# Keys and queries projected transposed and stacked through DRAM, in a fused attention and mixture-of-experts kernel

## What is computed

```python
q = (ln(x) @ Wq + bq)                      # 256 x 256, 16 heads of 16
k = concat([side @ Wk + bk, ctx], axis=1)  # 512 keys
v = concat([side @ Wv + bv, ctx], axis=1)
attn = softmax(einsum('bhqd,bhkd->bhqk', q, k) / 4)
x = x + (attn @ v) @ Wp + bp
h = ln(x)
cw = normalised(softmax(h @ w_router) * softmax(h @ w_gating / 0.1))   # 8 experts, all of them
x = x + sum_e cw[e] * ((silu(h @ w_gate[e]) * (h @ w_up[e])) @ w_down[e])   # hidden width 1024
```

## Time and profile before

| | |
|---|---|
| median of 3 runs | 2773.96 us (2772.17 to 2774.82) |
| profiled execution, its time | 2771.69 us |
| its span | 2769.6 us, granted TensorE clock 0.994 on average |
| busy share TensorE, VectorE, ScalarE, GpSimd | 98%, 73%, 61%, 62% |
| bytes moved | 252 MB |

### The profile page before, as it was taken

How to read it: one execution, slowest core, us unless ns; L and a number is a source line. 1 busy time by engine, 2 the same in 40 slices (tenths; PEclk the granted TensorE clock), 3 DMA queues, 4 the chain that set the end, 5 groups by cost and what they waited for, 6 DMA issues and landing times.

```text
span 2769.6 us, 48148 instructions
## 1 busy us (share of the span) xinstructions
PE 2721.2 (98%) x16465; PEld 2228.0 (80%) x16465; DVE 2009.8 (73%) x3254; ACT 1689.5 (61%) x3241; POOL 1720.9 (62%) x1886
## 2 busy tenths in 40 slices
PE   7789999999999999999999999999999999999998
PEld 5568888888888888888888888888888888888887
DVE  6877777768777777777777778677776867665554
ACT  7766666666666666565666666666666665544443
POOL 6766566666666566666665666665665665654554
PEclk9999999999999999999999999999999999999999
DMA  2113233332333322333232322323323233333332
GB/s 69 40 54 101 76 99 96 92 101 79 99 93 93 102 84 88 96 95 100 83 95 83 106 89 85 103 81 109 94 80 101 78 99 92 93 107 116 104 104 83
DMA packets 251280, 252.32 MB, mean 91 GB/s; under 512 B 15904, under 2 KB 242848, under 8 KB 251040
## 3 DMA queue, kind: packets, MB, share of 16 engines
q1 hardware_dynamic: 251040, 249.25, 29.6%
HBM read 240.66 MB, written 8.52 MB: 90 GB/s over the span
## 4 chain that ended last, share of the span: by engine, by line
PE 92%; issue 3%; DVE 2%; ACT 2%; POOL 1%; DMA 0%; SPq 0%; POOLq 0%; ACTq 0%; DVEq 0%
PE ps_t L670 25%; PE ps_o L704 24%; PE ps_s L670 24%; PE ps_s L764 4%; PE ps_t L774 4%; PE ps_m L549 3%; PE ps_a L746 2%; PE ps_a L748 2%; PE ps_m L607 1%; PE ps_m L567 1%; PE ps_m L622 1%; PE ps_m L614 1%; ACT Pt L928 0%; DVE Pt_lo L1154 0%; DVE negmax L1146 0%
## 5 line engine op out<-in xcount | busy, mean ns | idle before, releaser
L949 DVE SCALAR_TENSOR_TENSOR hf<-hf,ps_s 128x512 f32<-128x512 f32 x512 | 350.2, 684 | 401.5 <-ACT hf L788 400.3
L794 ACT ACTIVATE h_hi<-ps_t 128x512 fp32r<-128x512 f32 x512 | 306.2, 598 | 451.1 <-DVE ps_t L956 451.1
L961 DVE TENSOR_TENSOR h_lo<-ps_t,h_hi 128x512 fp32r<-128x512 f32 x512 | 353.0, 689 | 213.9 <-ACT h_hi L794 207.6
L788 ACT ACTIVATE hf<-ps_s 128x512 f32<-128x512 f32 x512 | 306.3, 598 | 329.8 <-PE ps_s L670 327.7
L1185 POOL TENSOR_TENSOR wg_lo<-stage_w,wg_hi 128x512 fp32r<-128x512 f32 x256 | 337.4, 1318 | 265.5 <-ACT wg_hi L801 264.7
L1250 POOL TENSOR_TENSOR Pt_lo<-Pt 128x512 f16<-128x512 f32 x256 | 289.7, 1132 | 197.9 <-ACT Pt L928 197.0
L704 PE MATMUL ps_o<-h_lo,wd_hi 128*128 128x512 f32 x1024 | 399.9, 390 | 0.0
L704 PE MATMUL ps_o<-h_hi,wd_hi 128*128 128x512 f32 x1024 | 398.5, 389 | 0.9 <-DVE h_lo L961 0.9
L704 PE MATMUL ps_o<-h_hi,wd_lo 128*128 128x512 f32 x1024 | 398.4, 389 | 0.0
L956 DVE TENSOR_TENSOR ps_t<-hf,ps_t 128x512 f32<-128x512 f32 x512 | 356.4, 696 | 48.1 <-PE ps_t L670 7.5
L1185 POOL TENSOR_TENSOR wd_lo<-stage_w,wd_hi 128x512 fp32r<-128x512 f32 x256 | 332.1, 1297 | 87.5 <-ACT wd_hi L801 87.5
(11 more groups left out here) (192 smaller groups left out, 5092.4 us busy)
## 6 DMA issues: line engine op xcount, KB each, us to landing
stage_w<-in_L_ffn_w_gate_dram SPq DMA_DIRECT2D x256, 256.0 KB, 2.7
stage_w<-in_L_ffn_w_up_dram SPq DMA_DIRECT2D x256, 256.0 KB, 3.0
stage_w<-in_L_ffn_w_down_dram SPq DMA_DIRECT2D x256, 256.0 KB, 2.7
cwb<-d_cw SPq DMA_DIRECT2D x64, 256.0 KB, 3.6
X<-in_x_dram SPq DMA_DIRECT2D x32, 256.0 KB, 3.2
C<-in_fside_BxSxS_dram SPq DMA_DIRECT2D x16, 256.0 KB, 3.0
KVM<-in_ctx_dram SPq DMA_DIRECT2D x16, 256.0 KB, 2.8
d_x<-X SPq DMA_DIRECT2D x16, 256.0 KB, 2.9
```

The costliest lines, as they stand in the source:

```text
L788: act.activation(hf[:], ps_g[:], ACT.Tanh, scale=0.5).then_inc(tanh_done, 1)
L794: act.activation(h_hi[f % FC][:], ps_u[:], ACT.Copy).then_inc(hh_done, 1)
L949: dve.scalar_tensor_tensor(out=hf[:], in0=hf[:], scalar=1.0, in1=ps_g[:], op0=ALU.add, op1=ALU.mult).then_inc(gate_done, 1)
L961: dve.tensor_tensor(h_lo[f % FC][:], ps_u[:], h_hi[f % FC][:].bitcast(F32), ALU.subtract).then_inc(hl_done, 1)
```

## The change

1. Keys and queries are projected with features on partitions (`project_across`: weights stationary, 256 tokens moving), so no transposition is needed. ScalarE evacuates the high part with the bias added from a per-partition column `bT`, VectorE the low part. The factor 1/4 goes into `Wq`'s split. Memory keys are transposed once per batch (item `m`, four transposes). Values have an item of their own (`v`).
2. The low and high parts are written to DRAM (`d_k`, `d_q`), 4 transfers per batch, and read back into the rows of `KTs` and `QTs`, for 4 pairs at once: 3 transfers of 32 partitions for keys, 6 of 16 partitions and one that clears the maxima's rows for queries, two groups per batch. `QTs` now holds all 8 pairs. Rows: slots of 32 (two heads of 16), the last 32 rows for the maxima. SP issues all of it.
3. `kT` and `qq` items are gone, `qm` (maxima only) stays. The other items stand at other steps. `kstack`, `qstack`, `KVM`'s key part, `QF` are gone.
4. In steps without feed-forward VectorE takes the low part of `Pt` (and the router's small work) ahead of the step's item and maximum, not behind.
5. Prologue: GpSimd clears all of `QTs`, a transfer fills the ones rows of `KTs`, `KEEP_BUSY` is set anew.

```diff
-        ITEMS = [(0, "kT", 5, 0), (1, "kT", 6, 0), (2, "qq", 1, 0), (3, "cT", 0, 1), (4, "kT", 7, 0), (5, "aT", 0, -1),
-                 (6, "qq", 2, 0), (8, "o", 0, -1), (9, "kv", 0, 1), (10, "qq", 3, 0), (11, "kv", 1, 1), (13, "xT", 0, 1),
-                 (14, "qq", 4, 0), (15, "x2T", 0, -1), (16, "q", 0, 1), (17, "lg", 0, -1), (18, "qq", 5, 0), (19, "kT", 0, 1),
-                 (20, "kT", 1, 1), (21, "y", 0, 0), (22, "qq", 6, 0), (23, "cwT", 0, -1), (24, "y", 1, 0), (25, "kT", 2, 1),
-                 (26, "qq", 7, 0), (27, "kT", 3, 1), (28, "kT", 4, 1), (30, "qq", 0, 1)]
-        FIRST_AT = {"cT": (1,), "xT": (2,), "kv": (4, 6), "q": (9,)}
+        ITEMS = [(1, "cT", 0, 1), (2, "qm", 1, 0), (4, "k", 0, 1), (5, "aT", 0, -1), (6, "qm", 2, 0), (8, "o", 0, -1),
+                 (9, "v", 0, 1), (10, "qm", 3, 0), (11, "xT", 0, 1), (12, "m", 0, 1), (13, "q", 0, 1), (14, "qm", 4, 0),
+                 (15, "x2T", 0, -1), (17, "lg", 0, -1), (18, "qm", 5, 0), (21, "y", 0, 0), (22, "qm", 6, 0),
+                 (23, "cwT", 0, -1), (24, "y", 1, 0), (26, "qm", 7, 0), (30, "qm", 0, 1)]
+        FIRST_AT = {"cT": (1,), "xT": (2,), "k": (4,), "m": (6,), "q": (7,), "v": (9,)}
...
+                eng.wait_ge(const_ready, CONSTS)
+                eng.dma_start(KTs[TOP:P].bitcast(F32), key_rows[TOP:P].unsqueeze(1).broadcast_to([ROWS, PAIRS, NK])).then_inc(rows_in, 16)
+            def store_keys(turn, d):
+                turn.wait(eng, k_l, d, 2)
+                turn.wait(eng, m_l, d, 1)
+                for n, part in enumerate((kT_hi, kT_lo)):
+                    eng.dma_start(d_k[turn.b + d, n].rearrange("(c p) n -> p c n", p=P), part[:].bitcast(F32)).then_inc(k_out.sem, 16)
...
+            def place_keys(turn, d, g):
+                turn.wait(eng, k_out, d, 32)
+                turn.wait(eng, t_ps, d - 1, 2 * OCT * (g + 1))
+                for slot, part in enumerate((0, 1, 0)):
+                    eng.dma_start(KTs[slot * ROWS:(slot + 1) * ROWS, g * GP:(g + 1) * GP, :].bitcast(F32),
+                                  d_k[turn.b + d, part, bass.ds(g * P, P)].rearrange("(a r) n -> r a n", r=ROWS)).then_inc(k_in[g].sem, 16)
+            def place_queries(turn, d, g):
+                turn.wait(eng, q_out, d, 32)
+                turn.wait(eng, t_ps, d - 1, 2 * OCT * (g + 1))
...
+                for slot, part in enumerate((0, 0, 1)):
...
+                    src = d_q[turn.b + d, part, bass.ds(g * P, P)].rearrange("(a h r) n -> h r a n", h=2, r=HD)
+                    for h in range(2):
+                        r = slot * ROWS + h * HD
+                        eng.dma_start(QTs[r:r + HD, pairs, h, :].bitcast(F32), src[h]).then_inc(q_in[g].sem, 32 if last and h == 1 else 16)
...
+                    first = turn.b == -1
+                    if turn.has(1) and step == (10 if first else 14):
+                        store_keys(turn, 1)
+                    if turn.has(1) and step == (10 if first else 15):
+                        store_queries(turn, 1)
+                    if turn.has(1) and step == (11 if first else 17):
+                        place_keys(turn, 1, 0)
+                    if turn.has(1) and step == (11 if first else 19):
+                        place_queries(turn, 1, 0)
+                    if turn.has(0) and step == 1:
+                        place_keys(turn, 0, 1)
+                    if turn.has(0) and step == 3:
+                        place_queries(turn, 0, 1)
...
-            KEEP_BUSY = {(-2, 0): 13, (-1, 2): 10, (-1, 4): 6, (-1, 19): 10, (-1, 22): 2, (-1, 24): 8}
+            KEEP_BUSY = {(-2, 0): 13, (-1, 2): 10, (-1, 4): 6, (-1, 24): 36}
...
+            def project_across(ps, col, a, w):
+                (act, act_lo), (wt, wt_lo) = a, w
+                for m in range(DC):
+                    n, last = 0, 3 * DC - 1
+                    for tok, half in ((act, wt), (act, wt_lo), (act_lo, wt)):
+                        for c in range(DC):
+                            mm = pe.matmul(ps[:, m * N:(m + 1) * N], half[:, c, col + m * P:col + (m + 1) * P], tok[:, c, :],
+                                           start=(n == 0), stop=(n == last))
+                            n += 1
+                return mm
...
-                        if i % 4 == 0:
-                            turn.wait(pe, kT_done, d, h // 2 + 1)
-                            turn.wait(pe, qT_done, d, 2 * (h // 2) + 2)
+                        if i % (4 * GP) == 0:
+                            g = i // (4 * GP)
+                            if turn.b + d == 0:
+                                pe.wait_ge(rows_in, 16)
+                            turn.wait(pe, k_in[g], d, k_in[g].per)
+                            turn.wait(pe, q_in[g], d, q_in[g].per)
...
+                    if f is None:
+                        router_weights(turn, step)
+                        low_part(turn, step)
                     name, k, d, one, _ = misc(turn, step)
...
+                    if turn.b == -1 and step == 4:
+                        dve.wait_ge(b_in[0], 32)
+                        dve.tensor_scalar(bT[:, 0], bT[:, 0], SCALE, None, ALU.mult).then_inc(b_scaled, 1)
...
-            pool.memset(kstack[:, :, 2, 3:HD].bitcast(F32), 0.0).then_inc(const_ready, 1)
-            pool.memset(kstack[:, :, 2, 0:3].bitcast(F32), 1.0).then_inc(const_ready, 1)
-            pool.memset(qstack[:, :, 2, :].bitcast(F32), 0.0).then_inc(const_ready, 1)
+            pool.memset(key_rows[:], 0.0).then_inc(rows_clear, 1)
+            pool.memset(QTs[:].bitcast(F32), 0.0).then_inc(const_ready, 1)
```

More of the change, by code:

```diff
@@ L30 @@
 P = 128
-SLOTS = 4
+ROWS = 32
 LN_EPS = 1e-5
@@ L296, in released @@
                 return [] if turn.closed is None else [(y_done, turn.closed * GB + k + 1)]
[L297 to L303, removed]
+            count, nth = {"qm": (qm_done, 2 * k + 2), "k": (k_l, 2), "m": (m_l, 1), "v": (v_done, 1), "xT": (xT_l, 1),
+                          "cT": (cT_l, 1), "aT": (aT_l, 1), "x2T": (x2T_l, 1), "q": (q_l, 2), "o": (x1_done, 1),
+                          "lg": (ldif_done, 1), "cwT": (cwT_done, 1)}[name]
             return [(count.sem, (b + d) * count.per + nth)] if turn.has(d) else []
@@ L597, in do_misc @@
                         pe.wait_ge(w_low, 2)
-                    project(ps, 0, 2 * D, (cT_hi, cT_lo), k, (wkv_hi, wkv_lo)).then_inc(kv_ps.sem, 1)
-                elif name == "kT":
+                    for t in range(QT):
+                        mm = project(ps, t * D, D, (cT_hi, cT_lo), t, (wkv_hi[:, :, D:2 * D], wkv_lo[:, :, D:2 * D]))
+                    mm.then_inc(v_ps.sem, 1)
+                elif name == "qm":
                     if turn.b == -1:
[L601 to L621, removed]
-                            mm = pe.transpose(ps[:, N + t * P:N + (t + 1) * P].bitcast(F32R),
-                                              stack_block(qstack, t, pair), ident_r[:])
-                        mm.then_inc(qT_ps.sem, 1)
+                        pe.wait_ge(ident_done, 3)
+                    turn.wait(pe, mq_l, d, k + 1)
+                    for t in range(QT):
+                        mm = pe.matmul(ps[:, t * P:(t + 1) * P], mq[k % 2][:, t, :], ident_b[:], start=True, stop=True)
+                    mm.then_inc(qm_ps.sem, 1)
                 elif name == "aT":
@@ new lines, in body @@
+                    if name in ("k", "q"):
+                        full, hi, out_c, b_at, used = {"k": (k_ps, kT_hi, k_h, 1, k_out), "q": (q_ps, qT_hi, q_h, 0, q_out)}[name]
+                        if turn.b == -1:
+                            act.wait_ge(*((b_in[1], 32) if name == "k" else (b_scaled, 1)))
+                        turn.wait(act, full, 1, 1)
+                        turn.wait(act, used, 0, 32)
+                        for m in range(DC):
+                            act.activation(hi[:, m, 0:N], ps[:, m * N:(m + 1) * N], ACT.Identity,
+                                           bias=bT[:, b_at, m:m + 1]).then_inc(out_c.sem, 1)
@@ new lines, in body @@
+                    if name == "m":
+                        turn.wait(act, m_ps, 1, 1)
+                        turn.wait(act, k_out, 0, 32)
+                        act.activation(kT_hi[:, :, N:NK], ps[:].rearrange("p (c n) -> p c n", n=N), ACT.Copy).then_inc(m_h.sem, 1)
+                    if name == "qm":
+                        turn.wait(act, qm_ps, d, k + 1)
+                        for h in range(2):
+                            act.activation(QTs[TOP:TOP + 3, k, h, :], ps[HS * h + ROWS:HS * h + ROWS + 3, 0:N],
+                                           ACT.Copy).then_inc(qm_done.sem, 1)
@@ L1031, in router_weights, with low_part @@
                                       ALU.mult).then_inc(cw_done.sem, 1)
+            def low_part(turn, step):
+                d, i = item_at(step, -1)
+                if turn.has(d) and by_dve(i):
+                    turn.wait(dve, exp_done, d, i + 1)
+                    slot = i % RING
```

(2 more changed lines are left out.)

206 lines of the change are left out of this document (86 added, 120 removed).

## The result

| | before | after |
|---|---|---|
| median, same chip | 2774.36 us | 2710.99 us (2710.2 to 2715.82) |
| ratio | | 0.9776, 95% interval 0.9764 to 0.9788 |
| profiled execution, its time | 2771.69 us | 2710.93 us |
| first key matmul | 26.55 us | 36.99 us |
| first gate of the feed-forward | 169.20 us | 166.50 us |

The kernel is 62 us faster by the ratio (59 to 65 us). Of the 60.5 us between the two spans, 57.8 lie behind the first gate and 2.7 ahead of it. Those 2.7 are a loss of 10.4 us in the prologue and a gain of 13.1 us in the attention-only turns (142.65 us from first key matmul to first gate before, 129.5 us after).

What follows compares the result with a forecast made beforehand. The prediction took TensorE, full in the joint stage (some 93% of the span), as the bound: 2771.7 - 55 (joint stage) + 0 (prologue and turns) = 2716.7 us, put at 2718 us for the median, range 2698 to 2744 us.

Steps and rivals of the forecast that it cites:

- The bound: Joint stage (one batch's attention woven into older ones' feed-forward): TensorE full, so work removed there is time; -55 us.
- key transposes: Joint stage: 104 items of four transposes leave TensorE at 0.39 us each, -40.6 us.
- query transposes: Joint stage: 104 items of two transposes leave TensorE at 0.15 us each, -15.6 us.
- added items: Joint stage, TensorE: memory-key transposes and separate key and value projections for 12 batches, +6.0 us.
- wait of step 18: Joint stage: ScalarE's wait for the last query transpose before building the query stack goes, -5 us, from 0 to 14.
- Transfers beside the joint stage at no cost: Writing and rereading keys and queries through DRAM adds about 7 points of queue share; nothing charged in the joint stage.
- Prologue: Before the first key matmul: DRAM writes and reads delay it to 33 to 36 us, +8 us, between +4 and +11.
- Attention-only turns: Before the joint stage: ScalarE's relief and the earlier low part return half of VectorE's idle time, -8 us, -13 to 0.
- A: Joint stage: a full tanh, VectorE and split loop behind TensorE keeps half of the 50 us away, about 2743 us; 10%.
- B: Joint stage: weight loads queue behind stores and placements, ScalarE's up split waits; 2795 us at 1.0 us each; 9%.
- C: B at a smaller price, or prologue near its upper end and steps 8 to 14 too dense: 2745 to 2772 us; 8%.
- D: Relief counts for more: query term 26.0 us, 10 us from step 18, turns at favourable end, 2698 us; 8%.

Runs made afterwards that it cites:

- e1: Kernel after with four useless key transposes put back on TensorE in 104 joint-stage steps, no copies or waits on a result: 2745.26 us.
- e2: Kernel before, from turn 3 on with one of four key and one of two query transposes per item, ScalarE's copies unchanged in size and number: 2746.52 us.
- e12: Kernel after with two useless query transposes ahead of the maxima's own in 104 joint-stage items, no ScalarE copies: 2733.25 us.
- e3: Kernel before with the query stack built one step later, at step 19 instead of 18: 2765.66 us.
- e9: Kernel after with 104 useless groups of four key transposes, each followed by a ScalarE copy that the next item waits for: 2744.9 us.
- e4: Kernel after, from turn 3 on reading each group of key rows from DRAM once more into a spare buffer: 2714.47 us.
- e5: Kernel after with VectorE's low part and the router's small work behind the maximum in every step, as before the change: 2718.4 us.
- e6: Kernel before with the low part moved ahead of the maximum in steps without feed-forward: ratio 0.9981 to before.

## Why the prediction was right, point by point

*The bound.* Right. The joint stage was TensorE's time, and e1, e2 and e12 show it from both sides. Joint stage in sum: forecast -55 us, measured -57.8. The third column has each term by an experiment, the fourth by the mean step lengths.

| term | forecast us | by experiment | by step lengths |
|---|---|---|---|
| key transposes | -40.6 | -34.9 (e1) | -36.8 |
| query transposes | -15.6 | -17 to -22.5 (e12) | -17.1 |
| added items | +6.0 | none | +5.9 |
| wait of step 18 | -5.0 | -5.1, up to -11 by timing (e3) | -6.3 |
| sum | -55 | -51 to -56.5 with +6.0 for the added items and -5.1 | -54.3 |

The key term was mis-sized: the difference of two single steps, 0.39 us, stood for 104 items, and one plain step in the earlier trace rows (4.56 us) was on the short side; plain steps after are 4.57 and 4.59 us, and the mean before was 4.58. The query term erred the other way, by 1.5 us if the step lengths are right and by 7 at most. That the sum came so close is in part luck: the key term was 4 to 6 us too large, and the query term, the wait of step 18 and a rest in no term made up for it. No experiment priced the added items; 5.9 us are a step with the memory keys against a plain one (0.45 us) and the two projections (0.04 us), for 12 batches. What the step lengths leave of the 57.8 us, 3.5 us, is spread: no other step of a turn is more than 0.06 us shorter. ScalarE's copies are excluded by e9 as a cause in this stage.

*Transfers beside the joint stage at no cost.* Right, and e4 shows room for more. The queue's share grew by 9.3 points (29.6% to 38.9%), where I had said about 7; nothing hung on it. The Trainium skill (SBUF — State Buffer, Door 1: The DMA port swizzle) had let me expect slower transfers into 32 partitions: the key rows' 256 KB land in 4.9 us at the median and weights of the same size over 128 partitions in 2.8 us, which agrees in its direction; but three such transfers are issued one behind the other, and even the first of the three (4.4 us at the median) has a weight load just ahead of it, so no row parts the ports from the queue.

*Prologue.* Forecast +8 us, between +4 and +11, first key matmul at 33 to 36 us; measured +10.4 us and 36.99. Clearing QTs was shorter than I had said (3.52, not 4.2 us; rstd at 6.7, not 8 us). It also delayed rstd by a way that I had not named: three small operations of VectorE (lines 1021 to 1023) took 1.67 to 1.81 us each while GpSimd was clearing, and 0.16 to 0.17 us in the kernel before. The low parts were ready about when I had said (13.2, 13.8 and 16.8 us). I took 3 us for a store to land; the key store took 7.3 and the later of the query stores 5.6 us, and the landing of the placements came at 29 and not at 26 to 28 us. I had not reckoned with the clock at 0.50 behind that gap either; the eight maxima needed 8.0 us, 0.6 more than the 7.4 of my sum.

*Attention-only turns.* Forecast -8 us, between -13 and 0; measured -13.1, just outside; between other traces of the same turns it is up to -18 (145.0 us in e2, 126.6 in e1). I had VectorE keep half of its idle time; it keeps 8.3 of 129.6 us. The low part ahead of the score's wait is shown as a reason, for 3 to 7 us (e5, e6); ScalarE's relief is not shown apart from the fewer items. Prologue and turns together: 0 forecast, -2.7 measured. Two errors of 2.4 and 5 us with opposite signs made that small.

*The rivals.* A (a full loop behind TensorE) is refuted by 500.00 of 500 us and by e2; B (late weights) by e4. Of C the prologue near its upper end came true, but the turns paid for it. D was in part what happened: the turns at their good end, and a query term of at most 22.5 of its 26.0 us. The time lies 7 us below the forecast, within the parts' ends: 2.8 us from the joint stage, 2.7 from what lies ahead of it, and most of the rest is the 1.3 us put on top because the profiled execution lay below the median, which it does not after the change.

*Small slips in the sums.* The ends +11 and 0 of prologue and turns add up to +11, not +10; the 2739 us use the 11. Half of B's 9% is 4.5%, so B alone does not give the 8% for slower. And 2716.7 + 2.3 is 2719, not 2718. None of these changes the argument.

## What to carry to other kernels

Where one engine is full for nine tenths of the span, price an edit by the work that leaves that engine, and check the price by putting the same work back without use: it costs one run and needs no undoing of the change. Take the price of a small operation on a full engine from several steps with and without it, not from one pair, and not from its own piece in the chain alone: 104 items of 0.29 us cost 0.34, and 104 of 0.15 cost 0.16 to 0.22 each. Averaged by their place in the turn, the step lengths of two traces give the same prices without a further run. A detour through DRAM can be free in the steady state and still cost 10 us once, where nothing runs yet that could hide its two landings.

## What the runs showed of the hardware that I had not expected

- The prologue's landings vary by 3 us between six kernels with the same transfers up to there, one execution each, on at least three chips (first score 28.97 to 32.08 us), more than the edits of it bring. The kernel before, whose first score waits for no store, has it at 18.14 to 18.42 us in four.
- 104 copies of 0.60 us on ScalarE, waited for by TensorE's next item, cost nothing measurable (0.4 us) in a stage where TensorE is full.
- The length of a step at one place of the turn repeats between executions: the 32 means of e6 and of the kernel before, whose joint stages are the same code, add up to 167.57 us in both.
- 20 MB more on the same queue, at 43.3% of the engines' time, did not change the landing of 256 KB of weights (2.8 us for gate and down, 3.1 for up, in both kernels).
